# Last head attention: the queries' squares summed by turning them and squaring with ACT's accumulator

## The chip, the cores and the metric

The kernel runs on one core of a Trainium2 chip, in one launch. The metric is the device time of that launch in microseconds (us). The engines are named as in the profile: PE is TensorE (PEld its weight loads), ACT is ScalarE, DVE is VectorE, POOL is GpSimd, SP issues the DMAs.

## The reference, cut to what matters

Four blocks of attention and feed-forward work on `x` of 32 x 64 x 512 and a context of the same size. The change touches the attention of the last block (its names carry the tag 3): 32 heads of 128 columns, 8 pairs of key and value heads, four query heads to each.

```python
def _rmsnorm(x, w):
    xf = x.astype(jnp.float32)
    var = jnp.mean(xf * xf, axis=-1, keepdims=True)
    return (xf * jax.lax.rsqrt(var + EPS)).astype(x.dtype) * w
q = (hidden_states @ Wq.T).reshape(bsz, q_len, H, HD).transpose(0, 2, 1, 3)
k = (cross_attention_states @ Wk.T).reshape(bsz, kv_len, KVH, HD).transpose(0, 2, 1, 3)
q = _rmsnorm(q, q_norm_w)
k = _rmsnorm(k, k_norm_w)
scores = jnp.einsum('bhqd,bhkd->bhqk', q, k) * scale + attention_mask
probs = jax.nn.softmax(scores, axis=-1)
out = jnp.einsum('bhqk,bhkd->bhqd', probs, v)
return out @ Wo.T
```

Each query row needs the sum of the squares of its 128 columns. The kernel folds the two weights of the norms into the keys and multiplies the finished scores of a row by its query's inverse root.

## The kernel before, in words

`phase_heads` runs twice, for the attention of the second block (tag 1, without norm) and for the last one (tag 3, `norm` true). Its outer loop takes four groups of 8 batches. In a group, `heads` goes over 8 key heads, each with four steps t = 0 to 3, so 32 steps n: a pair of query heads takes two steps, one for each half of the 8 batches. The bodies of the first and last key head are written out, those between them are a loop of the hardware. "Third step" below is t = 2, an odd step is t = 1 or 3.

The engines run their own fixed lists and meet by semaphores. PE's list is the one that sets the order. In step n it does, in this order:

- `scores(t)` (L1663), keys times queries for four batches, into bank SBK; two query heads lie in the 128 columns of one piece of `qf`;
- in the third step of all but the last key head `keys(i + 1)`, the next key head's projection (L131 to L133, twelve products);
- `head(n + 2)`, the query projection of a head two steps on, twelve products of 128x512 into bank QB (L131 to L133). ACT then squares QB into `sq` and copies it to `qf` (`head_high`, L1580 and L1581), and `a_q` counts it;
- `turn` (L1679), the previous step's softmax shares turned, which DVE copies to `tf` (L1791);
- `output` of two steps ago, twelve products with the output weights; in the third step it comes before `turn`;
- in odd steps `squares_sum` (L1673): eight products of `sq` with 32 columns of ones, into the free half of bank SBK, one sum of squares for each row of the next pair;
- `values_of` (L1687), the values' products of the previous step into bank AB.

ACT's list in a step: the exponential (L1607), `head_high`, in odd steps the high parts of the next weights (`wqh` L1540, `woh` L1545) and `queries_root` (L118 and L120: logarithm, exponential), then `out_high` (L1585), which takes the values' products. DVE multiplies the scores by the root (L1814), does the softmax (L1816 to L1830) and the low part of the output (`out_low`, L1795). POOL makes the low parts of the weights (L1516, L1520), SP loads them.

The waits around the change are these three, on PE before `scores`, on PE before `squares_sum`, and on DVE before the scaling:

```python
if norm and t % 2 == 0:
    pe.wait_ge(m["a_qrs"], 2 * (i * HP + t // 2) + 1)
pe.wait_ge(m["v_s"], n + 1)
dve.wait_ge(m["a_qrs"], 2 * (i * HP + t // 2) + 2)
```

Of the kernel before, what the change touches and what calls it, by code (L numbers as in the profile page):

```python
# [11 lines left out]
ALU = mybir.AluOpType  # L12
ACT = mybir.ActivationFunctionType
AX_X = mybir.AxisListType.X

P = 128
B, S, D = 32, 64, 512
BG = 8
# [37 lines left out]
def build(nc, a, out):  # L56
    with ExitStack() as top:
# [1344 lines left out]
        def heads(tag, g, NKV, HP, KEYS, norm, wq, wo, wk, vraw, rq, ro, rk, wqh, wql, wkh, wkl, keys_of, queries_of, craw, gate):  # L1402
# [5 lines left out]
            SCALE = float(HD) ** -0.5  # L1408
            names = ("s_q", "a_q", "s_k", "a_ksq", "s_kss", "s_qss", "v_kn", "a_kn", "a_k", "v_in", "s_s",
                     "v_s", "v_m", "a_e", "v_p", "s_t", "v_t", "s_av", "a_o", "v_o", "s_wo", "a_wq", "p_wq",  # L1410
# [3 lines left out]
            PT = 128 * (HB * KEYS // P)  # L1414
            EQ = 32
            with ExitStack() as ph:
                def tb(name, shape, dt=F32):
                    return sb(f"h{tag}_{name}", shape, dt, ctx=ph)
# [9 lines left out]
                if norm:  # L1428
                    sq, ksq, rks, sc = (tb("sq", [P, 2, BG, 2, S]), tb("ksq", [P, TG]), tb("rks", [P, TG]),
                                        tb("sc", [P, HB, KEYS]))  # L1430
                    qrs = tb("qrs", [P, 2, BG])

# [4 lines left out]
                def ring_of(z, n):  # L1437

                    return z[:, n // 2, :, n % 2, :]
# [10 lines left out]
                with nc.Block() as blk:  # L1450
# [80 lines left out]
                    def _(act):  # L1531
# [34 lines left out]

                        def queries_root(k, pair):

                            act.wait_ge(m["s_qss"], k + 1)
                            root(act, qrs[:, pair], ps[:, SBK, HB * KEYS:2 * HB * KEYS].rearrange("p (b e) -> p b e", e=EQ)[:, :, 0],  # L1570
                                 m["a_qrs"], 2 * k, 1.0 / HD, EPS, math.log(SCALE))

# [4 lines left out]
                        def head_high(n, ring):  # L1577
                            act.wait_ge(m["s_q"], n + 1)
                            if norm:
                                nc.scalar.activation(ring_of(sq, ring), by_batch(QB), ACT.Square)  # L1580
                            nc.scalar.copy(ring_of(qf, ring), by_batch(QB)).then_inc(m["a_q"], 1)  # L1581
# [14 lines left out]
                        head_high(1, 1)  # L1596
                        if norm:
                            queries_root(0, 0)

                        def body(i, first, last):  # L1600
                            for t in range(NS):
# [22 lines left out]
                                split_steps(act, i, t, last, kv, q, o)  # L1624
                                if norm and t % 2 and not (last and t == NS - 1):
                                    queries_root(i * HP + (t + 1) // 2, (t + 1) // 2 % 2)
                                if not (first and t == 0):
                                    out_high(n)
                        over_groups(act, body)
                        out_high(NSTEP)  # L1630

                    @blk.tensor
                    def _(pe):
# [33 lines left out]

                        def squares_sum(n, pair):

                            pe.wait_ge(m["a_q"], n + 2)  # L1670
                            for b in range(BG):
                                col = HB * KEYS + EQ * b
                                last = nc.tensor.matmul(ps[:, SBK, col:col + EQ], sq[:, pair, b].rearrange("p h t -> p (h t)"),  # L1673
                                                        ones[:, 0:EQ], start=True, stop=True)
                            last.then_inc(m["s_qss"], 1)

# [31 lines left out]
                        if norm:  # L1708
                            squares_sum(0, 0)

                        def body(i, first, last):
                            for t in range(NS):
# [6 lines left out]
                                if not start:  # L1719
                                    pe.wait_ge(m["v_s" if norm else "a_e"], n)  # L1720
                                if norm and t % 2 == 0:
                                    pe.wait_ge(m["a_qrs"], 2 * (i * HP + t // 2) + 1)
                                scores(t)
# [7 lines left out]
                                if not (last and t >= NS - 2):  # L1731
                                    pe.wait_ge(m["a_q"], n + 2)
                                    if t % 2 == 0:
                                        wait(pe, m["p_wq"], i * HP + t // 2)
                                    head(n + 2, t % 2, (t + 2) % 4, ((t + 2) // 2) % 2)
# [21 lines left out]
                                if not (first and t < 2) and not early:  # L1757
                                    product()
                                if norm and t % 2 and not (last and t == NS - 1):
                                    pe.wait_ge(m["v_s"], n + 1)  # L1760
                                    squares_sum(n + 1, (t + 1) // 2 % 2)
                                if not start:
# [17 lines left out]
                    def _(dve):  # L1780
# [27 lines left out]
                        def largest(i, t, own):  # L1808
                            n = i * NS + t
                            dve.wait_ge(m["s_s"], n + 1)  # L1810
                            if norm:
                                dve.wait_ge(m["a_qrs"], 2 * (i * HP + t // 2) + 2)
                                half = slice(HB * (t % 2), HB * (t % 2) + HB)
                                nc.vector.tensor_tensor(sc[:], kbank(SBK)[:, 0:HB], bc(qrs[:, t // 2 % 2, half]), ALU.mult).then_inc(m["v_s"], 1)  # L1814
                                dve.wait_ge(m["v_s"], n + 1)
# [145 lines left out]
```

## Time and profile before

| | us |
|---|---|
| median of 3 runs | 3870.94 |
| lowest and highest | 3866.55, 3883.64 |
| profiled execution, its own time | 3880.8 |
| its span, first to last instruction | 3879.0 |
| PE busy in the span | 3478.2 |
| ACT busy in the span | 1466.2 |
| mean granted TensorE clock | 0.946 of full |

The profiled execution has a span of 3879.0 us and 1.8 us around it. The last attention occupies the span from about 2409 us to 3797 us: four groups that look alike in the trace, with an entry stage (values of the context, norm of `x`) between them. In the profile a product of fp32 operands shows as two instructions, a turn as one; rows of `h_` names without a tag are of either attention, and the time tells which.

### The profile page before, as it was taken

To read this page: it belongs to the slowest core of one execution; us is meant where nothing else is said; L and a number is where in the kernel's file an instruction comes from. 1 tells how busy PE (TensorE), PEld (TensorE's weight loads), DVE (VectorE), ACT (ScalarE), POOL (GpSimd) and SP (SyncE) were. 2 spreads that over 40 slices of the span, in tenths; PEclk is the share of its full clock that TensorE was granted. 3 is DMA by queue.
4 is the path that set the end of the run, shared out by engine and by line. 5 is a ranking of instruction groups with operands and counts; after the bars stand their busy time and mean duration, and the time that the engine had idled before them with its cause. 6 is when DMAs were issued, how large, how long until landed. Compare 5 with 4: busy or idle time off the path is not lost. (4 is left out here: it accounts for less than half of the span.)

```text
span 3879.0 us, 50267 instructions
## 1 busy us (share of the span) xinstructions
PE 3478.2 (90%) x18456; PEld 2828.8 (73%) x18466; DVE 1768.3 (46%) x3589; ACT 1466.2 (38%) x3218; POOL 937.3 (24%) x515
## 2 busy tenths in 40 slices
PE   6999989799899899979988935999899999989996
PEld 5777775588688778868865723888588778868884
DVE  4677765234333424433443464444344434434444
ACT  3333432344244334434432443343344333433432
POOL 1111102233223223223322312222222222222220
PEclk8899999899999999999998977999999999999998
DMA  2000000221112122112101102210112121111111
GB/s 91 1 1 1 1 1 20 87 71 56 55 62 68 36 71 68 38 66 71 58 22 76 44 3 87 63 60 30 68 60 62 35 73 59 54 54 51 60 40 49
DMA packets 57162, 191.33 MB, mean 49 GB/s; under 512 B 9152, under 2 KB 9920, under 8 KB 53184
## 3 DMA queue, kind: packets, MB, share of 16 engines
q1 hardware_dynamic: 57024, 189.46, 14.5%
q8 instruction: 91, 1.49, 0.2%
q14 instruction: 47, 0.39, 0.0%
HBM read 185.24 MB, written 4.19 MB: 49 GB/s over the span
## 5 line engine op out<-in xcount | busy, mean ns | idle before, releaser
L1795 DVE TENSOR_TENSOR h_ol<-ps,h_oh 128x512 fp32r<-128x512 f32 x256 | 177.1, 692 | 743.2 <-ACT h_oh L1585 743.2
L1516 POOL TENSOR_TENSOR h_wql<-h_rq,h_wqh 128x1024 fp32r<-128x1024 f32 x112 | 276.2, 2466 | 937.7 <-ACT h_wqh L1540 937.7
L131 PE MATMUL ps<-h_woh,h_oh 128*128 128x512 f32 x1024 | 437.0, 427 | 23.5 <-DVE h_ol L1795 23.2
L133 PE MATMUL ps<-h_woh,h_ol 128*128 128x512 f32 x1024 | 405.1, 396 | 0.0
L132 PE MATMUL ps<-h_wol,h_oh 128*128 128x512 f32 x1024 | 403.6, 394 | 0.0
L1520 POOL TENSOR_TENSOR h_wol<-h_ro,h_woh 128x1024 fp32r<-128x1024 f32 x128 | 305.6, 2387 | 187.3 <-ACT h_woh L1545 187.3
L1585 ACT CAST h_oh<-ps 128x512 fp32r<-128x512 f32 x256 | 149.7, 585 | 445.7 <-PE ps L1687 445.7
L1791 DVE COPY h_tf<-ps 128x512 f32<-128x512 f32 (+1 forms) x256 | 142.7, 557 | 347.7 <-PE ps L1679 347.7
L1687 PE MATMUL ps<-h_tf,h_vf 128*128 128x128 f32 x2048 | 279.0, 279 | 17.6 <-DVE h_tf L1791 17.6
L1687 PEld LDWEIGHTS ps<-h_tf,h_vf 128*128 128x128 f32 x2048 | 262.0, 192 | 38.5 <-DVE h_tf L1791 25.2
L1610 ACT ACTIVATE h_ex<-ps,h_mx 128x128 f32<-128x128 f32 x512 | 181.4, 366 | 241.0 <-DVE h_mx L1821 241.0
L1663 PE MATMUL ps<-h_kf,h_qf 128*128 128x128 f32 (+1 forms) x2048 | 267.6, 274 | 4.1 <-ACT h_qf L1581 2.7
L1663 PEld LDWEIGHTS ps<-h_kf,h_qf 128*128 128x128 f32 x2048 | 252.7, 194 | 7.5 <-ACT h_qf L1581 4.4
L131 PEld LDWEIGHTS ps<-h_woh,h_oh 128*128 128x128 f32 x1024 | 192.8, 188 | 71.7 <-DVE h_ol L1795 30.7
L133 PEld LDWEIGHTS ps<-h_woh,h_ol 128*128 128x128 f32 x1024 | 193.2, 189 | 46.6
L132 PEld LDWEIGHTS ps<-h_wol,h_oh 128*128 128x128 f32 x1024 | 193.9, 189 | 42.3 <-issue 6.7
L131 PE MATMUL ps<-h_Hh,h_wqh 128*128 128x512 f32 x512 | 210.6, 411 | 13.9 <-POOL h_wql L1516 11.1
L131 PE MATMUL ps<-h_Xh,h_wqh 128*128 128x512 f32 x512 | 212.0, 414 | 2.5 <-ACT h_qf L1581 2.5
L133 PE MATMUL ps<-h_Xh,h_wql 128*128 128x512 f32 x512 | 204.0, 398 | 0.0
L132 PE MATMUL ps<-h_Xl,h_wqh 128*128 128x512 f32 x512 | 202.9, 396 | 0.0
L133 PE MATMUL ps<-h_Hh,h_wql 128*128 128x512 f32 x512 | 201.4, 393 | 0.0
L132 PE MATMUL ps<-h_Hl,h_wqh 128*128 128x512 f32 x512 | 201.0, 393 | 0.0
(278 smaller groups left out, 6938.3 us busy)
## 6 DMA issues: line engine op xcount, KB each, us to landing
h_rq<-in_L_Wq SPq DMA_DIRECT2D x128, 512.0 KB, 3.6
h_ro<-in_L_Wo SPq DMA_DIRECT2D x128, 512.0 KB, 4.0
h_rk<-in_L_Wk SPq DMA_DIRECT2D x48, 256.0 KB, 2.7
h_craw<-in_ctxT SPq DMA_DIRECT2D x10, 1024.0 KB, 5.5
cnat<-in_ctx SPq DMA_DIRECT2D x4, 1024.0 KB, 11.0
t_craw<-in_ctxT SPq DMA_DIRECT2D x4, 1024.0 KB, 4.9
t_cn<-in_ctx SPq DMA_DIRECT2D x4, 1024.0 KB, 6.1
out_rows<-x SPq DMA_DIRECT2D x16, 256.0 KB, 2.0
```

Source lines behind the costliest of these rows:

```text
L131: nc.tensor.matmul(dst, lh, rh, start=start, stop=False, **kw)
L132: nc.tensor.matmul(dst, lh, rl, start=False, stop=False, **kw)
L133: return nc.tensor.matmul(dst, ll, rh, start=False, stop=stop, **kw)
L1516: nc.gpsimd.tensor_tensor(wql[:, par], rq[:, par], f(wqh[:, par]), ALU.subtract).then_inc(m["p_wq"], 1)
L1520: nc.gpsimd.tensor_tensor(wol[:, par], ro[:, par], f(woh[:, par]), ALU.subtract).then_inc(m["p_wo"], 1)
L1585: nc.scalar.copy(by_head(oh), ps[:, AB, :].rearrange("p (b h t) -> p b h t", h=2, t=S)).then_inc(m["a_o"], 1)
L1610: ins = nc.scalar.activation(ex[:, b], kbank(SBK)[:, b], ACT.Exp, bias=mx[:, 1, b:b + 1], scale=SCALE, accum_out=mx[:, 2, b:b + 1])
L1663: last = nc.tensor.matmul(ps[:, SBK, b4 * KEYS:(b4 + 1) * KEYS], qf[:, pair, b].rearrange("p h t -> p (h t)"), kf[:, b], start=True, stop= ...
L1687: last = nc.tensor.matmul(ps[:, AB, b4 * P:(b4 + 1) * P], vf[:, b], tf[:, c * P:(c + 1) * P], start=True, stop=True)
L1791: nc.vector.tensor_copy(tf[:], ps[:, TBK, 0:PT]).then_inc(m["v_t"], 1)
L1795: nc.vector.tensor_tensor(by_head(ol), ps[:, AB, :].rearrange("p (b h t) -> p b h t", h=2, t=S), f(by_head(oh)), ALU.subtract).then_inc(m[ ...
```

## The change

The sums of squares of the queries are formed in another way, in every step and not in every second one.

- Gone: the Square of 128x512 in `head_high`; `squares_sum` on PE with its two waits; the wait of `scores` for the root.
- New on PE: `turn_queries(t + 1)` in each step between `output` (in the third step: `turn`) and `values_of`. Four transposes put the next step's queries, row by row, into bank QB. Before it PE waits for the copy of `head(n + 2)`.
- New on ACT: `queries_square(n + 1)` at the end of the step, behind `out_high`: four Squares of 128x128 out of QB, each with its sum into one column of `qss`; then `queries_root(n + 1)` on 4 columns.
- New wait on PE: `head(n + 2)` writes QB, so it waits for the four sums of `a_qsq`.
- DVE scales with the root of its own step.

```diff
-                        def queries_root(k, pair):
-
-                            act.wait_ge(m["s_qss"], k + 1)
-                            root(act, qrs[:, pair], ps[:, SBK, HB * KEYS:2 * HB * KEYS].rearrange("p (b e) -> p b e", e=EQ)[:, :, 0],
-                                 m["a_qrs"], 2 * k, 1.0 / HD, EPS, math.log(SCALE))
+                        def queries_square(n, half):
+                            act.wait_ge(m["s_qt"], n + 1)
+                            for b in range(HB):
+                                nc.scalar.activation(sq[:, half, b], ps[:, QB, b * HD:(b + 1) * HD], ACT.Square,
+                                                     accum_out=qss[:, b:b + 1]).then_inc(m["a_qsq"], 1)
+
+                        def queries_root(n, half):
+
+                            act.wait_ge(m["a_qsq"], HB * n + HB)
+                            root(act, qrs[:, half], qss[:], m["a_qrs"], 2 * n, 1.0 / HD, EPS, math.log(SCALE))
...
                         def head_high(n, ring):
                             act.wait_ge(m["s_q"], n + 1)
-                            if norm:
-                                nc.scalar.activation(ring_of(sq, ring), by_batch(QB), ACT.Square)
                             nc.scalar.copy(ring_of(qf, ring), by_batch(QB)).then_inc(m["a_q"], 1)
...
                                 split_steps(act, i, t, last, kv, q, o)
-                                if norm and t % 2 and not (last and t == NS - 1):
-                                    queries_root(i * HP + (t + 1) // 2, (t + 1) // 2 % 2)
                                 if not (first and t == 0):
                                     out_high(n)
+                                if norm and not (last and t == NS - 1):
+                                    queries_square(n + 1, (t + 1) % 2)
+                                    queries_root(n + 1, (t + 1) % 2)
...
-                        def squares_sum(n, pair):
-
-                            pe.wait_ge(m["a_q"], n + 2)
-                            for b in range(BG):
-                                col = HB * KEYS + EQ * b
-                                last = nc.tensor.matmul(ps[:, SBK, col:col + EQ], sq[:, pair, b].rearrange("p h t -> p (h t)"),
-                                                        ones[:, 0:EQ], start=True, stop=True)
-                            last.then_inc(m["s_qss"], 1)
+                        def turn_queries(t):
+
+
+                            for b4 in range(HB):
+                                last = nc.tensor.transpose(ps[:, QB, b4 * P:(b4 + 1) * P],
+                                                           qf[:, t // 2 % 2, HB * (t % 2) + b4].rearrange("p h t -> p (h t)"),
+                                                           ident[:])
+                            last.then_inc(m["s_qt"], 1)
...
-                                if norm and t % 2 == 0:
-                                    pe.wait_ge(m["a_qrs"], 2 * (i * HP + t // 2) + 1)
                                 scores(t)
...
                                     pe.wait_ge(m["a_q"], n + 2)
+                                    if norm:
+                                        pe.wait_ge(m["a_qsq"], HB * n + HB)
...
-                                if norm and t % 2 and not (last and t == NS - 1):
-                                    pe.wait_ge(m["v_s"], n + 1)
-                                    squares_sum(n + 1, (t + 1) // 2 % 2)
+                                if norm and not (last and t == NS - 1):
+                                    if not (last and t == NS - 2):
+                                        pe.wait_ge(m["a_q"], n + 3)
+                                    else:
+                                        pe.wait_ge(m["a_qsq"], HB * n + HB)
+                                    turn_queries(t + 1)
...
-                                dve.wait_ge(m["a_qrs"], 2 * (i * HP + t // 2) + 2)
-                                half = slice(HB * (t % 2), HB * (t % 2) + HB)
-                                nc.vector.tensor_tensor(sc[:], kbank(SBK)[:, 0:HB], bc(qrs[:, t // 2 % 2, half]), ALU.mult).then_inc(m["v_s"], 1)
+                                dve.wait_ge(m["a_qrs"], 2 * n + 2)
+                                nc.vector.tensor_tensor(sc[:], kbank(SBK)[:, 0:HB], bc(qrs[:, t % 2]), ALU.mult).then_inc(m["v_s"], 1)
```

ACT's list in the fourth step of a key head of the loop and the start of the next one, before and with the change (`h_ex` exponential, `h_kf` keys, `h_qf` queries' copy, `h_wqh` and `h_woh` weights, `h_qrs` root, `h_oh` output):

```order
L1607 ACTIVATE h_ex<-h_sc 128x256
L1561 COPY h_kf<-h_kn 128x512
L1578 REGISTER_ALU
L1580 ACTIVATE h_sq<-ps 128x8x64
L1581 COPY h_qf<-ps 128x8x64
L41 ISA
L1540 CAST h_wqh<-h_rq 128x1024
L1545 CAST h_woh<-h_ro 128x1024
L118 ACTIVATE h_qrs<-ps 128x8
L119 REGISTER_ALU
L120 ACTIVATE h_qrs<-h_qrs 128x8
L1585 CAST h_oh<-ps 128x4x2x64
```

```order
L1610 ACTIVATE h_ex<-h_sc 128x256
L1560 COPY h_kf<-h_kn 128x512
L1582 REGISTER_ALU
L1583 COPY h_qf<-ps 128x8x64
L41 ISA
L1539 CAST h_wqh<-h_rq 128x1024
L1544 CAST h_woh<-h_ro 128x1024
L1587 CAST h_oh<-ps 128x4x2x64
L1569 ACTIVATE h_sq,h_qss<-ps 128x128 x4
L1574 ISA
L118 ACTIVATE h_qrs<-h_qss 128x4
L119 ISA
```

The Square in front of the copy of `h_qf` is gone, the root has moved behind `h_oh`, and four Squares with sums stand ahead of it.

PE's list at the same place, from the end of `output` to the first product of the next `head`, before and with the change (here a product counts once; `h_tf` are the turned shares, `h_Xh` the normed rows):

```order
L133 MATMUL ps<-h_woh,h_ol 128x512
L1670 REGISTER_ALU
L1673 MATMUL ps<-ones,h_sq 128x32 x8
L1687 MATMUL ps<-h_tf,h_vf 128x128 x4
L1465 REGISTER_ALU
L1465 COMPARE_AND_BRANCH
L1663 MATMUL ps<-h_kf,h_qf 128x64 x4
L131 MATMUL ps<-h_Xh,h_wqh 128x512
```

```order
L133 MATMUL ps<-h_woh,h_ol 128x512
L1766 REGISTER_ALU
L1676 MATMUL ps<-ident,h_qf 128x128 x4
L1691 MATMUL ps<-h_tf,h_vf 128x128 x4
L1464 REGISTER_ALU
L1464 COMPARE_AND_BRANCH
L1667 MATMUL ps<-h_kf,h_qf 128x64 x4
L131 MATMUL ps<-h_Xh,h_wqh 128x512
```

Four turns stand where the eight narrow products stood; in even steps they are new, with nothing gone. Between the turns and the `head` that overwrites their bank stand the values' products and `scores`.

## Rows read from the trace of the kernel before

**Rows 1.** The page's head and its first part (busy us, share of the span).

```profile
span 3879.0 us, 50267 instructions
...
PE 3478.2 (90%) x18456; PEld 2828.8 (73%) x18466; DVE 1768.3 (46%) x3589; ACT 1466.2 (38%) x3218; POOL 937.3 (24%) x515
```

**Rows 2.** Busy time by stretch: length, PE, PEld, DVE, ACT, POOL, PEclk, DMA share, GB/s.

```profile
2442.00:2700.00 258.00, 254.38 (x1440) 216.38 (x1439) 114.67 (x265) 103.16 (x194) 68.89 (x33) 1.00 0.18 56
...
2420.00:2440.00 20.00, 17.12 (x93) 14.95 (x93) 6.90 (x18) 7.72 (x16) 3.50 (x2) 0.83 0.06 16
```

**Rows 3.** Waits of PE's loads, 2442 to 2700: waiter, releaser, total us, times, longest.

```profile
PEld ps L1687 <- DVE h_tf L1791: 5.3, 7, 0.8
```

**Rows 4.** Timeline of a body step's PE work: start us, us, engine, line, operation.

```profile
2592.63 0.48 PE L131 MATMUL ps<-h_ch,h_wkh 128*128 128x512 f32 x1
...
2595.47 0.39 PE L131 MATMUL ps<-h_Xh,h_wqh 128*128 128x512 f32 x1
...
2603.64 0.97 PEld L1663 LDWEIGHTS ps<-h_kf,h_qf 128*128 128x128 f32 x8
...
2610.20 1.98 PEld L1673 LDWEIGHTS ps<-ones,h_sq 128*128 128x128 f32 x16
...
2612.10 0.97 PEld L1687 LDWEIGHTS ps<-h_tf,h_vf 128*128 128x128 f32 x8
...
2613.00 0.97 PEld L1663 LDWEIGHTS ps<-h_kf,h_qf 128*128 128x128 f32 x8
...
2619.79 1.05 PE L1687 MATMUL ps<-h_tf,h_vf 128*128 128x128 f32 x8
...
2620.57 0.97 PEld L1663 LDWEIGHTS ps<-h_kf,h_qf 128*128 128x128 f32 x8
...
2621.47 0.19 PEld L131 LDWEIGHTS ps<-h_Xh,h_wqh 128*128 128x128 f32 x1
```

**Rows 5.** Timeline of PE's weight loads in the first attention: four turns, next load.

```profile
1306.40 0.58 PEld L1679 LDWEIGHTS ps<-ident,h_pr 128*128 128x128 f32 x4
...
1306.95 0.19 PEld L131 LDWEIGHTS ps<-h_woh,h_oh 128*128 128x128 f32 x1
```

**Rows 6.** ACT: two groups by line (xcount, busy us, mean ns), four timeline rows.

```profile
L118 ACT ACTIVATE h_qrs<-ps 128x8 f32<-128x8 f32 x64 | 11.4, 179 | 43.6 <-PE ps L1673 43.6
...
L1580 ACT ACTIVATE h_sq<-ps 128x512 f32<-128x512 f32 x128 | 75.8, 592 | 76.3 <-PE ps L133 76.0
...
2607.84 0.59 ACT L1580 ACTIVATE h_sq<-ps 128x512 f32<-128x512 f32 x1
...
2608.33 0.57 ACT L1581 COPY h_qf<-ps 128x512 f32<-128x512 f32 x1
...
2610.68 1.04 ACT L1545 CAST h_woh<-h_ro 128x1024 fp32r<-128x1024 f32 x1 [0.84 <-PE ps L133]
...
2620.88 0.59 ACT L1585 CAST h_oh<-ps 128x512 fp32r<-128x512 f32 x1 [2.84 <-PE ps L1687]
```

**Rows 7.** Timeline of ACT in the first attention: exponentials with accumulated sums.

```profile
1305.94 0.37 ACT L1610 ACTIVATE h_ex<-ps,h_mx 128x128 f32<-128x128 f32 x1 [2.05 <-DVE h_mx L1821]
...
1306.29 0.36 ACT L1610 ACTIVATE h_ex<-ps,h_mx 128x128 f32<-128x128 f32 x1
...
1307.23 0.22 ACT L1610 ACTIVATION_READ_ACCUMULATOR h_ex<-ps,h_mx 128x1 f32 x1
```

**Rows 8.** Timeline of PE's weight loads at a group's entry.

```profile
2421.19 1.86 PEld L1673 LDWEIGHTS ps<-ones,h_sq 128*128 128x128 f32 x16 [1.59 <-ACT h_qf L1581]
...
2423.49 1.78 PEld L1663 LDWEIGHTS ps<-h_kf,h_qf 128*128 128x128 f32 x8 [0.44 <-issue]
...
2425.15 0.33 PEld L131 LDWEIGHTS ps<-h_Xh,h_wqh 128*128 128x128 f32 x1
...
2430.06 1.22 PEld L1663 LDWEIGHTS ps<-h_kf,h_qf 128*128 128x128 f32 x8
...
2431.75 0.19 PEld L131 LDWEIGHTS ps<-h_Xh,h_wqh 128*128 128x128 f32 x1 [0.46 <-ACT h_qf L1581]
```

More of the change, by code:

```diff
@@ L1408, in heads @@
             SCALE = float(HD) ** -0.5
-            names = ("s_q", "a_q", "s_k", "a_ksq", "s_kss", "s_qss", "v_kn", "a_kn", "a_k", "v_in", "s_s",
+            names = ("s_q", "a_q", "s_k", "a_ksq", "s_kss", "s_qt", "a_qsq", "v_kn", "a_kn", "a_k", "v_in", "s_s",
                      "v_s", "v_m", "a_e", "v_p", "s_t", "v_t", "s_av", "a_o", "v_o", "s_wo", "a_wq", "p_wq",
@@ L1414, in heads @@
             PT = 128 * (HB * KEYS // P)
-            EQ = 32
             with ExitStack() as ph:
@@ L1428, in heads @@
                 if norm:
-                    sq, ksq, rks, sc = (tb("sq", [P, 2, BG, 2, S]), tb("ksq", [P, TG]), tb("rks", [P, TG]),
+                    sq, ksq, rks, sc = (tb("sq", [P, 2, HB, HD]), tb("ksq", [P, TG]), tb("rks", [P, TG]),
                                         tb("sc", [P, HB, KEYS]))
-                    qrs = tb("qrs", [P, 2, BG])
+                    qss, qrs = tb("qss", [P, HB]), tb("qrs", [P, 2, HB])
                 def values_raw(i, r):
@@ L1597, in _ @@
                         if norm:
+                            queries_square(0, 0)
                             queries_root(0, 0)
@@ L1708, in _ @@
                         if norm:
-                            squares_sum(0, 0)
+                            pe.wait_ge(m["a_q"], 2)
+                            turn_queries(0)
                         def body(i, first, last):
```

## The prediction

> **What bounds the kernel now.** I read four views in this order. The page's first part says that TensorE (PE) is busy 90% of the span [rows 1]. The stretches then say where: inside the last head attention it is busy 254.38 of 258 us at full clock, in one group of batches out of four alike, while ACT is busy only 103 us there [rows 2]. The waits in that stretch leave PE one stall, 5.3 us in 7 times, 0.76 us each, before the values' products in the third step of every head group, until DVE has copied the turned shares [rows 3]. So in this phase the queue of PE is the clock: what PE issues less is gained whole, what ACT does more costs nothing as long as PE doesn't wait for it. The timeline of PE's weight loads gives the pitch. From one `scores` to the next it is 9.36 us in an odd step, which holds `squares_sum`, and 7.57 us in an even one [rows 4].
>
> **What goes away on PE.** A `squares_sum` is 16 instructions (8 products, two passes each). They hold the queue 1.90 us, from 2610.20 to 2612.10. The difference of the two pitches is 9.36 − 7.57 = 1.79 us; I take that, since the values' products behind them start 0.1 us closer [rows 4]. A group of batches has 16 of these: one in the entry, one in step 1, and 14 in steps 3, 5, ... 29. The 14 give back 14 × 1.79 = 25.1 us. In step 1 it stood behind a wait for the copy; without it, and with the copy earlier, I reckon 1.8 us gained there, the new turn included.
>
> **What PE gets.** Each step now turns four 128x128 pieces of the queries. The first attention turns four such pieces in 0.55 us, from 1306.40 to 1306.95 [rows 5]. Behind a large product the next small block starts about 0.1 us closer, as above, so 0.45 us a step. In the seven third steps they fall into the 0.76 us that PE waits anyway [rows 3] and cost nothing; if DVE's copy came sooner they would cost their 0.55. That leaves 22 steps of the body: 22 × 0.45 = 9.9 us.
>
> **What ACT gets, and who waits.** ACT loses one Square of 128x512 per step, 0.59 us [rows 6], and does four Squares of 128x128 with a sum, plus the root in every step and not in every second. ACT has the room. But the order counts: the turned queries lie in the PSUM bank into which the next `head` writes, and PE now waits for all four sums (`a_qsq`) before that `head`. ACT may start the Squares only behind `out_high`, which waits for the values' products. So the chain is: values done, `out_high`, four Squares, `head`; what PE has to do meanwhile is `scores` alone. In numbers, from the row of the values' products: they end at 2619.79 + 1.05 = 2620.84 and the next `head` loads at 2621.47, so PE has 0.63 us of cover behind that end [rows 4]. `out_high` starts 0.04 us after the end [rows 6]. The next ACT operation on its heels starts 0.49 us later, as Square and copy do at 2607.84 and 2608.33 [rows 6].
>
> The four Squares are the unknown. Upper bound: the four exponentials with a sum of the first attention run from 1305.94 to the end of the last accumulator read at 1307.23 + 0.22 = 1307.45, 1.51 us at a pitch of 0.35 [rows 7]. They take their bias from a tensor, the Squares don't. From the rows of ACT's operations out of PSUM without such a bias, 0.179 us for 8 columns and 0.592 for 512 [rows 6], 128 columns lie at 0.179 + 120/504 × 0.413 = 0.28 us. In rows 7 the pitch is about the duration (0.35 against 0.37), so 3 × 0.28 + 0.28 + a last read's end 0.1 later, 1.2 us. That is my value, nearer in kind; lower bound 1.0, if the reads overlap more. The stall is then 0.04 + 0.49 + 1.2 + 0.04 (semaphore to PE) − 0.63 = 1.14, say **1.15 us**; with 1.51 it is 1.45, with 1.0 it is 0.95. The Trainium skill (ScalarE: Activation LUTs, What ACT_TABLE_LOAD costs) says that a bias given as a pointer adds about 93 ns to an ACTIVATE. By that page as an estimate the exponentials' chain less 4 × 0.09 is 1.15 us, and the sum below would come out at about +20 us instead of the +51 us that the exponentials' own row gives.
>
> Which steps pay? A group has 30 `head` calls in its steps. In the seven third steps `keys` stands between `scores` and `head`, 2.84 us of products (2592.63 to 2595.47) [rows 4], more than any bound. Two belong to the entry. 21 pay: 21 × 1.15 = 24.2 us. Other users don't wait longer: the softmax of a step needs the root, about 0.5 us behind the sums, which puts its start 0.5 us behind the start of `head`. Today it starts about 0.7 us behind it, because DVE's `out_low` comes first. The product's split weights have the whole of `head` as cover. In an odd step `woh` starts at 2610.68 and takes 1.04 us [rows 6]; the values' products would end at 2610.20 + 0.55 + 1.2 = 2611.95, so `out_high` is not held, with 0.2 us to spare.
>
> **Entry and end of a group.** At the entry PE waits for the copy of the second head, then sums, and the first `scores` waits for the root. That chain stands at 2421.19, 2423.49 and 2425.15 [rows 8]. Now the copy comes 0.49 earlier, four turns take 0.55, `scores` waits for nothing, and the next `head` waits for the Squares: 2420.70 + 0.55 + 0.2 + 1.2 = 2422.65, 2.5 us sooner. The head after it, 6.6 us behind today (2431.75), gets the whole round trip, copy 0.6, turn 0.55, Squares 1.2 and three handovers, about 1.4 us more. Net −1.1. At the end the last two softmaxes start 1.3 us later, of which the waits for `out_low` that are there today cover all but 0.3.
>
> **Sum.** Per group: −25.1 − 1.8 + 9.9 + 24.2 − 1.1 + 0.3 = +6.4 us; four groups: **+25 us** (25.6). Against the profiled execution's own 3880.8 us that is 3906; the profiled execution is 10 us above the median of the runs, so I put the same difference on the median of 3870.9: **3896 us**, +0.65%. A measurement of this kernel can tell about 0.5%, some 19 us, from no change; the forecast lies just beyond.
>
> **Rivals.**
> *The Squares cost what the exponentials cost* (stall 1.45): 0.3 × 21 × 4 = 25 us more, 3921. For it: the only rows with a sum of this size. Against it: the bias.
> *Not slower: the cover is longer and the entry keeps its clock.* In the entry the clock is granted at half for a while: the stretch from 2420 to 2440 shows 0.83 [rows 2], `scores` takes 1.78 us instead of 0.97, and the twelve products of `head` from 2425.15 to 2430.06 take 4.9 us, where the twelve of `keys` in the body take 2.84 [rows 4, 8]. With turns of 128 columns in place of the 32 column sums, and no wait for the root, PE may stay at 2.4 GHz there. Half clock costs 0.17 × 20 = 3.4 us in that stretch; I count three quarters of it as won back, 2.6 us more per group, an entry of −3.7. With that, the sum is zero at a stall of (25.1 + 1.8 − 9.9 + 3.7 − 0.3)/21 = 0.97, about the lower bound; at 0.95 it is −2 us, 3869. It decides by the Squares' chain: under 1.03 us no loss, over it a loss. For it: the reads may hide; against it: in rows 7 each read holds the next exponential back.
> *The stall is hidden altogether*, if the Squares in fact run beside something PE still has to do: then only the gains are left, 4 × (6.4 − 24.2) = −71, 3800. Against it: the order on both engines.
> *The clock.* Both attentions' bodies are granted the full 2.4 GHz without a break, with 1.8 us of 32 column sums in every second step; with turns and an idle PE instead, it may fall to 1.2 GHz as in the entry, where PE had waited and then run narrow products. One fall costs about 0.17 × 20 = 3.4 us [rows 2]; one per pass over four steps is 28 × 3.4 = 95 us on top of the forecast, 3991. For it: idle time comes to every step. Against it: the first attention turns four pieces a step at full clock, and stalls here are 1.15 us between blocks of wide products. The Trainium skill (TensorE: Matmul & The Clock Gate, Part 4: PE-mode transpose) states that transposes don't count as PE activity the way products do. By that page the turns would be idle time for the clock, next to the stall.
>
> **Numbers.** Chances: forecast 0.50, dear Squares 0.17, not slower 0.20, stall hidden 0.07, clock 0.06. The forecast's own spread (stall 1.0 to 1.3, turns 0.35 to 0.55) is about 13 us each way, so a third of it lies within 0.5%. Slower by over 0.5%: 0.33 + 0.17 + 0.06 = 0.56; within: 0.17 + 0.20 = 0.37; faster: 0.07. The range takes in both bounds of the Squares and leaves out the hidden stall, the clock and some tails: 3870 to 3930.
>
> **What would show it.** In the changed profile: no 128x32 products; 512 more transposes, in blocks of four at about 0.55 us; four Squares of about 0.28 us with reads at a pitch near 0.28; PE waits for them before `head` 21 times in a group for about 1.1 us, and not in the step with `keys`; the even pitch of `scores` near 7.57 + 0.45 + 1.15 = 9.2 us, the odd one the same; granted clock 1.00 in the body. If the waits are under 0.9 us or absent, or if the clock in the body isn't 1.00, the forecast is wrong in that step.

## The result, and the profile after

Over 22 runs of each kernel the medians are 3869.07 us before (3852.31 to 3883.64) and 3885.16 us after (3866.25 to 3896.42). The ratio is 1.0042 with an interval of [1.0028, 1.0055]: 16 us slower. That is less than the 25 us forecast, with its sign and inside its range. One of the five runs of experiment 7 below took 5910 us at a granted clock of 0.55; its cause is open, and the ratio there leaves it out (the median does not).

The two profiled executions can't be subtracted. That of after took 3875.96 us, 4.8 us less than that of before, although the four groups of its last attention are 13.8 us longer together: everything else, which both kernels share, came out 18.6 us shorter. So I compare stretches of the last attention. The page's head and first part, after:

```profile
span 3874.2 us, 50460 instructions
...
PE 3407.7 (88%) x17944; PEld 2744.0 (71%) x17954; DVE 1799.4 (46%) x3589; ACT 1572.2 (41%) x4242; POOL 944.7 (24%) x515
```

PE has 512 matmuls less and is busy 70.5 us less than in [rows 1]. ACT has 1024 instructions more and is busy 106 us more. So PE was given time back, and the kernel is no faster. Groups by line and form say where the time went (count, then busy us, mean ns, then idle time before and what ended it):

```profile
L131 PE MATMUL ps<-h_Xh,h_wqh 128*128 128x512 f32 x512 | 209.9, 410 | 80.3 <-ACT h_sq L1569 76.6 <-issue 3.7
L1569 ACT ACTIVATE h_sq<-ps 128x128 f32<-128x128 f32 x512 | 134.9, 285 | 6.0 <-PE ps L1676 6.0
L1569 ACT ACTIVATION_READ_ACCUMULATOR h_sq<-ps 128x1 f32 x512 | 110.4, 216 | 0.0
```

The product of `head` now stands 76.6 us behind the Squares (L1569), a wait that before did not have. The stretch that answers to [rows 2], and the waits in 2442 to 2700 that answer to [rows 3]:

```profile
2440.00:2700.00 260.00, 241.66 (x1320) 201.45 (x1319) 119.07 (x264) 122.39 (x405) 67.74 (x31) 1.00 0.17 50
```

```profile
PE ps L131 <- ACT h_sq L1569: 16.3, 18, 1.0
...
PEld ps L131 <- ACT h_sq L1569: 12.2, 12, 1.0
PEld ps L131 <- issue: 9.0, 13, 1.1
PEld ps L1691 <- DVE h_tf L1799: 1.9, 6, 0.3
```

PE is busy 93% of this stretch where it was busy 99% of the other [rows 2], at a granted clock of 1.00 in both. Part of the loads' stall is listed as "issue": seven of those 13 times it is the same wait, of 1.0 to 1.1 us ahead of `head`, and the other six are 0.24 us each ahead of `output`, as in before. The old wait for DVE's copy has shrunk from 0.76 us to 0.3 us, since the turns now use up the rest. One step of the body, the `scores` of an odd step (2603.38) with what stands around them, in PE's loads and then in ACT's timeline:

```profile
2601.93 0.59 PEld L1676 LDWEIGHTS ps<-ident,h_qf 128*128 128x128 f32 x4
2602.49 0.97 PEld L1691 LDWEIGHTS ps<-h_tf,h_vf 128*128 128x128 f32 x8
2603.38 0.97 PEld L1667 LDWEIGHTS ps<-h_kf,h_qf 128*128 128x128 f32 x8
2605.37 0.19 PEld L131 LDWEIGHTS ps<-h_Xh,h_wqh 128*128 128x128 f32 x1 [1.01 <-ACT h_sq L1569]
...
2611.02 0.59 PEld L1676 LDWEIGHTS ps<-ident,h_qf 128*128 128x128 f32 x4
```

```profile
2603.69 0.58 ACT L1587 CAST h_oh<-ps 128x512 fp32r<-128x512 f32 x1 [3.77 <-PE ps L1691]
2604.17 0.28 ACT L1569 ACTIVATE h_sq<-ps 128x128 f32<-128x128 f32 x1
2604.34 0.20 ACT L1569 ACTIVATION_READ_ACCUMULATOR h_sq<-ps 128x1 f32 x1
2604.43 0.28 ACT L1569 ACTIVATE h_sq<-ps 128x128 f32<-128x128 f32 x1
...
2605.09 0.23 ACT L1569 ACTIVATION_READ_ACCUMULATOR h_sq<-ps 128x1 f32 x1
```

ACT waits 3.77 us for the values' products, then runs `out_high` first. The four Squares run from 2604.17 to 2605.09 + 0.23 = 2605.32, and 0.05 us later PE loads for `head`. Turned queries had been in the bank since about 2602.5. ACT stood idle while they were ready, because `out_high` comes first in its list.

**Where the 13.8 us are.** From the times at which PE starts `scores`, the stretches of a group of batches (us, mean of the four groups). A group is counted from PE's first products in it (of zeros, L1636 in before) to the end of its last `output`; the values of the context and the norm of `x` between two groups are left out. The first row ends at the `scores` of step 2, each other one at the next `scores`:

| stretch of a group | before | after | after − before |
|---|---|---|---|
| entry, steps 0 and 1 | 28.92 | 23.47 | −5.45 |
| step 2 | 12.44 | 13.23 | +0.8 |
| steps 3 to 29 | 255.81 | 263.22 | +7.4 |
| step 30 | 5.36 | 5.81 | +0.45 |
| from there to the end of the group | 15.62 | 15.86 | +0.24 |
| group | 318.14 | 321.59 | +3.4 |

The four groups of after agree within 0.1 us (321.55 to 321.61). Those of before don't: 318.14, 316.51, 316.57 and 321.35. They differ by the clock. In 18 us at the entry it was 0.81, 0.91, 0.91 and 0.81, and in the fourth group it fell once more in steps 1 and 2:

```profile
3500.00:3518.00 18.00, 16.92 (x74) 14.35 (x75) 5.19 (x13) 6.99 (x14) 5.89 (x3) 0.81 0.23 73
```

There step 2 takes 13.91 us, in the other three groups 11.95. Against those three the change costs 1.3 us in step 2, and the +0.8 is a mean with a group in which the clock of before had fallen. The kernel of experiment 4, whose PE list is that of before, lacks this second fall in its profile; its groups are 0.85 us shorter in the mean. From them the change costs 4.3 us a group, 17 us in all. So the 13.8 us are known to about 3 us.

In the body the pitches of `scores` are 9.10 in odd steps (9.37 before), 9.18 in even ones (7.57) and 11.93 in the third (11.94).

Two stretches differ from the forecast: the entry gained more, and step 2 lost something. At the entry, after:

```profile
2402.05 0.42 PEld L1676 LDWEIGHTS ps<-ident,h_qf 128*128 128x128 f32 x4 [1.10 <-ACT h_qf L1583]
2402.44 0.97 PEld L1667 LDWEIGHTS ps<-h_kf,h_qf 128*128 128x128 f32 x8
2404.00 0.19 PEld L131 LDWEIGHTS ps<-h_Xh,h_wqh 128*128 128x128 f32 x1 [0.59 <-issue]
...
2407.71 0.42 PEld L1676 LDWEIGHTS ps<-ident,h_qf 128*128 128x128 f32 x4 [1.10 <-ACT h_qf L1583]
```

`scores` takes 0.97 us, not 1.78, and the twelve products of `head` end within 2.7 us, not 4.9 [rows 8]. The stretches of 18 us around the first group's entry give the clock as 0.81 in before and 1.00 in after:

```profile
2418.00:2436.00 18.00, 15.16 (x67) 12.33 (x65) 6.84 (x17) 5.26 (x13) 0.00 (x0) 0.81 0.09 38
```

```profile
2400.00:2418.00 18.00, 15.23 (x88) 12.34 (x87) 9.11 (x20) 10.66 (x40) 4.09 (x3) 1.00 0.14 50
```

In step 2, after (POOL, DVE, ACT and PE in the order of their starts):

```profile
2417.69 2.39 POOL L1519 TENSOR_TENSOR h_wol<-h_ro,h_woh 128x1024 fp32r<-128x1024 f32 x1
...
2418.29 2.07 DVE L1823 TENSOR_TENSOR h_sc<-h_sc,mask 128x256 f32<-128x256 f32 x1
...
2421.31 0.42 ACT L1610 ACTIVATE h_ex<-h_sc 128x256 f32<-128x256 f32 x1 [3.58 <-DVE h_sc L1825]
...
2422.32 0.30 PEld L1655 LDWEIGHTS ps<-h_ksq,ones 128*128 128x128 f32 x2 [1.45 <-issue]
```

The mask addition takes 2.07 us where its neighbours of the same size take 0.42. It ends 0.28 us behind the end of POOL's instruction (2420.36 and 2420.08). Behind it the exponential is late, behind that ACT's work on the keys (L1579), and PE waits 1.45 us. Before had the same hold in its first three groups, earlier against PE's work (the addition ends 4.05 us behind the start of the step's `scores`, after 5.72), and no wait of PE behind it. Its first group:

```profile
2440.05 2.40 POOL L1520 TENSOR_TENSOR h_wol<-h_ro,h_woh 128x1024 fp32r<-128x1024 f32 x1
...
2440.68 2.06 DVE L1816 TENSOR_TENSOR h_sc<-h_sc,mask 128x256 f32<-128x256 f32 x1
```

### The profile page after: what moved, and what is told of

It reads as the page before. It is cut to its first block and busy times, and to the rows that moved or that the text cites. A ratio compares the mean times of both kernels' runs of the same rounds, so it can differ in the third digit from the quotient of the medians.

```text
span 3874.2 us, 50460 instructions
## 1 busy us (share of the span) xinstructions
PE 3407.7 (88%) x17944; PEld 2744.0 (71%) x17954; DVE 1799.4 (46%) x3589; ACT 1572.2 (41%) x4242; POOL 944.7 (24%) x515
## 5 line engine op out<-in xcount | busy, mean ns | idle before, releaser
L1515 POOL TENSOR_TENSOR h_wql<-h_rq,h_wqh 128x1024 fp32r<-128x1024 f32 x112 | 282.5, 2522 | 932.9 <-ACT h_wqh L1539 932.9
L131 PE MATMUL ps<-h_Xh,h_wqh 128*128 128x512 f32 x512 | 209.9, 410 | 80.3 <-ACT h_sq L1569 76.6
L131 PE MATMUL ps<-h_Hh,h_wqh 128*128 128x512 f32 x512 | 210.8, 412 | 13.8 <-POOL h_wql L1515 11.1
L1544 ACT CAST h_woh<-h_ro 128x1024 fp32r<-128x1024 f32 x128 | 133.9, 1046 | 179.0 <-PE ps L133 162.2
```

The lines of the kernel that those rows point to most:

```text
L131: nc.tensor.matmul(dst, lh, rh, start=start, stop=False, **kw)
L1515: nc.gpsimd.tensor_tensor(wql[:, par], rq[:, par], f(wqh[:, par]), ALU.subtract).then_inc(m["p_wq"], 1)
L1544: nc.scalar.copy(woh[:, par], ro[:, par]).then_inc(m["a_wo"], 1)
```

## The experiments

Theory: the body's loss is one wait per step, for a chain that begins with `out_high`, and the gain lies at the entry, where the clock stays up. Rivals: ACT's added work or the turns cost by themselves; the bank is what costs, in whatever order ACT works; the entry gained only because a wait is gone.

**1. The Squares ahead of `out_high`.**

```diff
+    queries_square(n + 1, (t + 1) % 2)
     out_high(n)
-    queries_square(n + 1, (t + 1) % 2)
     queries_root(n + 1, (t + 1) % 2)
```

> The changed kernel with one move: ACT does the four Squares ahead of out_high and the root behind it. Theory A (the loss is the round trip: out_high, Squares, then head, with only scores as cover; 1.1 us in each of 21 steps of a group): the Squares now run beside the values' products, the wait of PE before head goes in even steps and falls to about 0.3 us behind an odd step, where the cast of woh comes first; 4 x 21 x 1.1 = 92 less about 17 left over, so 75 us less than the changed kernel's 3885, about 3810, ratio to before 0.985. Pitch of scores 8.0 us where the step before was even, 8.3 where it was odd. Theory B (the loss is the extra work itself, turns on PE and ACT's load): no move, ratio stays at 1.004.

Measured: 3807.91 us (5 runs), 0.9833 [0.9812, 0.9855] of the 3873.85 of before. Odd pitch 8.02, even 8.35, third unchanged at 11.93, a group 301.2 us. PE's loads in an even step and at the start of the next, then ACT's timeline:

```profile
2623.60 0.97 PEld L1668 LDWEIGHTS ps<-h_kf,h_qf 128*128 128x128 f32 x8
2624.85 0.19 PEld L131 LDWEIGHTS ps<-h_Xh,h_wqh 128*128 128x128 f32 x1 [0.28 <-issue]
...
2631.97 0.97 PEld L1668 LDWEIGHTS ps<-h_kf,h_qf 128*128 128x128 f32 x8
2632.86 0.19 PEld L131 LDWEIGHTS ps<-h_Xh,h_wqh 128*128 128x128 f32 x1
```

```profile
2631.38 0.28 ACT L1569 ACTIVATE h_sq<-ps 128x128 f32<-128x128 f32 x1 [2.82 <-PE ps L1677]
...
2632.30 0.22 ACT L1569 ACTIVATION_READ_ACCUMULATOR h_sq<-ps 128x1 f32 x1
2632.40 0.60 ACT L1587 CAST h_oh<-ps 128x512 fp32r<-128x512 f32 x1
```

The Squares now run beside the values' products and `scores`, and in the odd step `head` starts 0.89 us after `scores`, with no wait. The move of two lines takes 77 us off the change by the medians, 81 us by the two ratios and by the traces (4 × 20.4). Of the 23.1 us that a group had lost in its 21 steps (1.10 us each, worked out below), 21.0 came back; what is left is the 0.28 us in even steps, where the cast of `woh` stands ahead of the Squares. Step 30 is 0.7 us longer than in after (6.51 against 5.81). So nearly the whole loss in the body was the order on ACT, not the amount of its work. A second measurement on another chip gave the same:

> sq_first again beside pool_pieces on one chip, to tell their 5 us apart: theory (step 2 is 1.27 us shorter in pool_pieces, nothing else differs) gives pool_pieces a ratio lower by 0.0013; the rival gives none.

Measured: 3809.33 us (6 runs), 0.983 [0.9792, 0.9868].

**2. Every Square twice.**

```diff
+    for b in range(HB):
+        nc.scalar.activation(sq[:, 1 - half, b], ps[:, QB, b * HD:(b + 1) * HD], ACT.Square,
+                             accum_out=spare[:, b:b + 1])
     for b in range(HB):
         nc.scalar.activation(sq[:, half, b], ...
```

> The changed kernel with each set of four Squares done twice on ACT (the first set into a spare sum). Theory A (ACT's chain between out_high and head is exposed in full in 21 steps of a group): 4 more at 0.25 us are 1.0 us a step, 84 us in all, ratio to before about 1.026; the third step, where keys covers, stays at 11.93 us. Theory B (the waits are a handover of fixed length and ACT has room): under 10 us.

Measured: 4049.65 us (4 runs), 1.0445 [1.0424, 1.0465], more than expected. The size per Square was as expected: a paying step grows by 1.04 us (9.18 to 10.2 at t = 0, 9.10 to 10.17 at t = 1), and the third step stays at 11.93. That is about 22 us of the 41 that a group grew by. Most of the rest goes with the clock. A stretch of the body, and one step's load with its wait:

```profile
2780.00:3080.00 300.00, 259.61 (x1269) 204.91 (x1268) 108.38 (x238) 149.05 (x581) 72.71 (x35) 0.95 0.18 55
```

```profile
2860.18 0.19 PEld L131 LDWEIGHTS ps<-h_Xh,h_wqh 128*128 128x128 f32 x1 [2.13 <-issue]
```

At 2.1 us of idle time in three of four steps the granted clock in the body is 0.95, no longer 1.00, and in most passes over the four steps the pitch at t = 3 becomes 11.7, now and then the one at t = 0 too, where 10.2 shows without a fall: 1.5 us. The entries fell too, to 0.91, 0.75, 0.74 and 0.91 over 18 us. So the mechanism of the prediction's clock rival exists, and the change's own body, with 1.1 us of idle time in three of four steps, doesn't meet it.

**3. Every turn twice.**

```diff
-    for b4 in range(HB):
+    for b4 in 2 * list(range(HB)):
         last = nc.tensor.transpose(ps[:, QB, ...
```

> The changed kernel with the four turns of the queries done twice in each step. Theory A (PE's queue is full, a turn costs its load's pitch of 0.14 us): 0.56 us in 22 steps, 0.25 us in the seven third steps where 0.32 us of idle time is left, and the entry twice 0.56: 15 us a group, 60 us in all, ratio to before about 1.020. Theory B (turns fall into the time that PE waits for ACT anyway): near 0, ratio 1.004.

Measured: 3940.12 us (4 runs), 1.0151 [1.0123, 1.0178]. In the trace the four groups are 45 us longer than in after, where 60 was expected: four more turns cost 0.43 us in a step that pays (9.10 to 9.53), not 0.56, and 0.11 in the third, not 0.25. In the block of eight:

```profile
2605.31 1.03 PEld L1676 LDWEIGHTS ps<-ident,h_qf 128*128 128x128 f32 x8
2606.30 0.97 PEld L1691 LDWEIGHTS ps<-h_tf,h_vf 128*128 128x128 f32 x8
```

A block of four holds the queue 0.56 us, one of eight 0.99, so a further turn costs 0.11 us. The turns are a real cost with the size that the prediction gave them, and no second stall hangs on them.

**4. ACT's work alone, in the kernel before.** Four Squares with sums of `ident` behind `out_high`, and the root in every second step more; nobody waits for them.

```diff
     out_high(n)
+    for b in range(HB):
+        nc.scalar.activation(spsq[:, t % 2, b], ident[:], ACT.Square,
+                             accum_out=spare[:, t % 2, b:b + 1]).then_inc(m["a_x"], 1)
+    act.wait_ge(m["a_x"], HB * n + HB)
+    if t % 2 == 0:
+        root(act, spq[:, t // 2], spare[:, 0], m["a_y"], ...)
```

> The kernel before with ACT's new work alone: behind out_high of each step four Squares of 128x128 with sums, of the identity and into spare tiles, and a root in even steps too; nobody waits for them. Theory A (ACT's added load costs nothing, only who waits for it does): ratio 1.000, pitches of scores 7.57, 9.37 and 11.94 us as before. Theory B (ACT's load holds its other operations back): 0.3 us or more a step, 30 us or more.

Measured: 3872.56 us (10 runs) beside 3873.85, 0.9999 [0.9976, 1.0023]; the pitches are those of before to 0.01 us (7.57, 9.37, 11.94). ACT is busy 1638.0 us in this profile, 172 us more than in before and 66 more than in after, and that is free as long as nobody waits for it. With experiment 1 this excludes the first rival.

**5. The turned queries in another bank.** ACT's list is the change's own; the turns go to bank TBK, and PE waits for the Squares before `keys` and before `turn` instead of before `head`. Before `turn_queries` it waits for DVE's copy of TBK.

```diff
-    ps[:, QB, b4 * P:(b4 + 1) * P]
+    ps[:, TBK, b4 * P:(b4 + 1) * P]
```

> The changed kernel with the turned queries in the bank of the turned shares instead of the bank of head; head no longer waits for the Squares, but keys (third step), the next turn of shares and, for DVE's copy, the turn of the queries do. ACT's order stays (out_high first). Theory A (what costs is that the next head overwrites the bank): pitches of scores 8.02 us in three of four steps instead of 9.1; the third step now pays the 1.1 us before keys and about 0.5 us behind DVE's copy, 13.5 instead of 11.93. 37.6 instead of 39.3 us for four steps, 12 us a group, about 48 us less than the changed kernel's 3885, ratio to before 0.992. Theory B (ACT's order alone costs, whoever overwrites what): ratio stays at 1.004.

Measured: 3834.27 us (6 runs), 0.9916 [0.9891, 0.9941] of the 3871.18 of before. Pitches 8.01 and 8.26, the third 13.49. Two waits of a third step, in PE's loads:

```profile
2610.78 0.19 PEld L131 LDWEIGHTS ps<-h_ch,h_wkh 128*128 128x128 f32 x1 [1.02 <-ACT h_sq L1569]
...
2621.00 0.42 PEld L1676 LDWEIGHTS ps<-ident,h_qf 128*128 128x128 f32 x4 [0.82 <-issue]
```

In odd and even steps `head` now covers the Squares and the stall is gone. The 0.24 us that an even step still takes over an odd one are another wait, for POOL's low part of the query weights (L1515), which `head` reads. It ends 0.06 us before `head` loads:

```profile
2628.99 2.36 POOL L1515 TENSOR_TENSOR h_wql<-h_rq,h_wqh 128x1024 fp32r<-128x1024 f32 x1 [16.48 <-ACT h_wqh L1539]
```

```profile
2630.29 0.97 PEld L1667 LDWEIGHTS ps<-h_kf,h_qf 128*128 128x128 f32 x8
2631.41 0.19 PEld L131 LDWEIGHTS ps<-h_Xh,h_wqh 128*128 128x128 f32 x1
```

In the third step it stands before `keys`, which uses the same bank, and a second one comes with DVE's copy. So it is a matter of how much work PE has between the turns and the next writer of their bank. Either more of it or an earlier Square cures it; the earlier Square of experiment 1 costs 0.7 us a group in step 30 and nothing in the third step.

**6. The entry, in three kernels.** The narrow products put back, with nobody waiting for them:

```diff
     pe.wait_ge(m["a_q"], 2)
+    for b in range(BG):
+        col = HB * KEYS + 32 * b
+        nc.tensor.matmul(ps[:, SBK, col:col + 32], ...qf[:, 0, b]..., ones[:, 0:32], start=True, stop=True)
     turn_queries(0)
```

> The changed kernel with eight 128x32 products of the queries with ones (results unused) ahead of the first turn at each group's entry, as squares_sum stood there. Theory A (the entry kept its full clock because these narrow products and the wait for the root are gone): the clock at the entry falls to half again, the first step's pitch goes from 5.65 to 6 us or more and the stretch shows PEclk under 1; the group grows by more than the products' 1.9 us. Theory B (the clock there is chance or hangs on what came before): only 1.9 us a group, PEclk 1.00.

The wait of the first `scores` for the root put back:

```diff
+    if norm and start:
+        pe.wait_ge(m["a_qrs"], 2)
     scores(t)
```

> The changed kernel with the old wait alone: the first scores of a group wait for the root of the first queries. Theory A (idle time at the entry lets the clock fall): first pitch over 6 us and half clock in at least some groups, plus about 2 us of waiting a group. Theory B (the narrow products alone do it): 2 us a group of waiting, clock 1.00.

And both:

> The changed kernel with both, the eight narrow products and the wait for the root at a group's entry. If they act together, as in the kernel before, half clock shows at all four entries; if only chance decides, at some.

Measured, one execution each: 3890.32, 3891.40 and 3901.88 us. A single total can't tell these apart, but a group's time in the trace can (us; the body's steps 3 to 29 are 263.2 to 263.7 in the first four kernels of the table, 255.8 in before):

| kernel | the four groups | granted clock in 18 us at the entry |
|---|---|---|
| after | 321.6 in each | 1.00 in each |
| products back | 324.9, 325.4, 323.8, 323.8 | 0.91 in the first two, 1.00 in the last two |
| wait back | 324.5 in each | 0.91 in each |
| both back | 327.2 in each | 0.81 in each |
| before | 318.1, 316.5, 316.6, 321.4 | 0.81, 0.91, 0.91, 0.81 |

The windows' lines behind it, of the kernel with the products (first and third group), with the wait, and with both:

```profile
2400.00:2418.00 18.00, 15.57 (x89) 12.85 (x88) 7.86 (x18) 8.22 (x29) 1.30 (x2) 0.91 0.07 29
3129.00:3147.00 18.00, 15.22 (x95) 12.71 (x94) 8.23 (x19) 9.30 (x32) 2.38 (x2) 1.00 0.07 27
```

```profile
2403.00:2421.00 18.00, 13.92 (x75) 11.22 (x73) 7.69 (x18) 8.58 (x29) 1.67 (x2) 0.91 0.05 19
```

```profile
2406.00:2424.00 18.00, 14.32 (x70) 11.48 (x68) 5.18 (x14) 5.96 (x26) 0.00 (x0) 0.81 0.06 23
```

Either of the two alone lowers the clock at least in some groups, both together bring it down to 0.81 in all four, which before shows in two. In the profiles of after and of experiments 1, 3, 5 and 7, which have neither, all entries kept 1.00. So PE stays at 2.4 GHz here because both are gone, the wait and the narrow products; in the kernels of this experiment that rests on four entries in one execution of each. Putting them back costs a group 2.2 to 5.6 us, their own time included. What the clock alone costs can be read in the kernel with the products, whose groups differ by it: step 0 takes 6.81 and 7.24 us where the clock fell to 0.91, and 5.64 where it stayed, 1.2 to 1.6 us.

**7. POOL's instruction in pieces.** Experiment 1 with the weights' low part of step 1 in four pieces of 256 columns:

```diff
+    if norm and type(n) is int and n == 1:
+        for h in range(2):
+            for c in range(2):
+                k = slice(256 * c, 256 * c + 256)
+                ins = nc.gpsimd.tensor_tensor(wol[:, par, h, k], ro[:, par, h, k], f(woh[:, par, h, k]), ALU.subtract)
```

> The kernel sq_first with POOL's subtraction of the second product weights in the first key head cut into four pieces of 256 columns. Theory A (in step 2 DVE's mask addition, 2.07 us instead of 0.43, is held until POOL's 2.39 us instruction ends, and PE waits for what follows): the addition takes 1 us or less and the pitch of step 2 falls from 13.2 to about 12 us, 5 us in all, ratio to before 0.982. Theory B (DVE's operation is slow there for another reason): 2 us again, pitch 13.2.

Measured: step 2 falls from 13.22 to 11.96 us, a group from 301.2 to 299.95. POOL's and DVE's timelines:

```profile
2410.52 3.27 POOL L1523 TENSOR_TENSOR h_wol<-h_ro,h_woh 128x256 fp32r<-128x256 f32 x4
...
2411.17 0.42 DVE L1831 TENSOR_TENSOR h_sc<-h_sc,mask 128x256 f32<-128x256 f32 x1
```

The mask addition runs 0.42 us beside POOL's 3.27 us, and PE's wait is gone. That is worth 5 us over the four groups in the trace, although the four pieces take POOL longer than the one instruction did, and it is below what the totals can tell: 3802.77 us (5 runs), 0.9837 [0.9794, 0.9881]. A second measurement, beside experiment 1:

> pool_pieces again beside sq_first_b: ratio to before 0.982, 5 us less than sq_first_b, if the four shorter steps reach the end; the same time if they don't.

Measured: 3793.81 us (6 runs), 0.9801 [0.9763, 0.9839], beside 0.983 [0.9792, 0.9868] for experiment 1 on the same chip. The intervals overlap; that the pieces gain in the total is not shown, that they remove the hold in step 2 is. With either version the kernel beats both before and the change: 1.7 to 2% under before and 2 to 2.4% under the change.

## Why the prediction was right, and where it missed

- **What bounds the kernel.** Right. PE's queue is the clock: 172 us more of ACT are free where nobody waits for them (experiment 4), and turns that hold the queue 0.43 us longer make the pitch 0.43 us longer (experiment 3).
- **The products that go, 14 × 1.79.** Right. With the turns at 0.45 and without a stall the odd pitch is 9.37 − 1.79 + 0.45 = 8.03; experiment 1 shows 8.02.
- **The turns, 0.45 in the step.** Right, by the same pitch. In even steps 7.57 + 0.45 = 8.02 stands against 8.26 in experiment 5 and 8.35 in experiment 1, with a wait ahead of `head` in both: for POOL's part of the weights in experiment 5, for the Squares behind the cast of `woh` in experiment 1.
- **The stall, 21 × 1.15.** Right in place and size. It is 9.10 − 8.03 = 1.07 in odd steps and 9.18 − 8.02 = 1.16 in even ones, mean 1.10. The Squares' chain is 2605.32 − 2604.17 = 1.15 us, not 1.2, since their pitch is 0.25 and not 0.28. The third step doesn't pay, as forecast. Steps 3 to 29 came to +7.4 per group; the terms give 21 × (0.45 + 1.15) − 25.1 = +8.5.
- **Entry and step 1: the term that was mis-sized.** The prediction put −1.1 and −1.8, together −2.9. The traces show −5.45, so 2.5 us per group or 10 us in all were missed. I took the instructions one by one at the speed at which before ran them, and left the granted clock to a rival. Step 1 was right: 8.5 us before, at full clock in the second and third group, and 6.55 after. The −1.1 of the entry was right too but for the clock: in these two groups the stretch up to the `scores` of step 1 is 2.4 us shorter, and of that their fall to 0.91 is worth 1.2 to 1.6 us, an estimate from experiment 6. The rival's entry with step 1, −3.7 − 1.8 = −5.5, is the measured mean, in part by luck: it took the first group's lower clock for all four, where the groups gained 5.9, 4.3, 4.3 and 7.2 us, the fourth with its second fall. The rival's other half, a stall of 0.95, is not what was measured.
- **Step 2: a term that was missing, +0.8 in the mean, +1.3 where before ran it at full clock.** The softmax of step 1 is late now and falls under POOL's instruction in a place where PE waits for what follows. The hold is in the trace of before too, with nobody waiting behind it; I costed the later softmax only at a group's end.
- **The ends.** Step 30 +0.45 as forecast, the tail +0.24 against 0.3.

With the measured values the sum is 7.4 − 5.45 + 0.8 + 0.45 + 0.24 = +3.4 per group and +13.8 for the four, and 16 us in the totals, interval 11 to 21. The forecast of 25 had the stall right, and was too high by the entry. It came within 9 us of the totals partly by luck: the two terms that it missed, the clock at the entry and the hold in step 2, have opposite signs. At 16 us, under the 19 that bound "within 0.5%", it was that case that held, to which I gave 0.37 against 0.56 for slower by more.

Of the other rivals: dear Squares fell at 1.15 against 1.51 us. A hidden stall fell, and experiment 1 shows what it would have been worth: the prediction's 3800 us for that case against a measured 3808. The clock falling in the body didn't occur at 1.1 us of idle time in three of four steps, and did at 2.1. The Trainium skill (TensorE: Matmul & The Clock Gate, Part 4: PE-mode transpose) states that transposes don't count as activity of PE the way products do; in the body here that made no difference, as 1.00 was granted with four turns in each step and a stall in three of four.

## What to carry to other kernels

When an engine hands a shared bank back to the engine that sets the pace, what counts is the chain from the last work it waits for to the release, and not how busy it is. List what stands between in its in-order queue: here one 0.48 us copy ahead of the release, a copy that itself waits for products which end later than the turns that were ready, turned a gain of some 65 us into a loss of 16. And cost a stretch that runs at the lower clock at both clocks: taking a wait out of it can give back more than the wait.

## What the runs showed of the hardware

- **A VectorE addition is held by a GpSimd instruction until that one ends.** With both inputs in SBUF, 128x256 takes 2.07 us beside a GpSimd subtraction of 2.39 us, which it outlasts by 0.28 us, and 0.42 us without, or when the latter is cut in four. The Trainium skill (SBUF — State Buffer, Who interferes with whom) states that a DVE instruction with two SBUF inputs contends with a GpSimd instruction that reads SBUF; this trace agrees, and the pieces (3.27 us in all, the addition 0.42) show that the length of the single GpSimd instruction is what counts.
- **TensorE's granted clock at an entry depends on small things.** With the wait for the root or with eight narrow products it fell to 0.91 over 18 us, with both to 0.81; with neither it stayed at 1.00, except where the Squares were done twice and PE waited longer there (0.74 to 0.91). With the products alone it differed between groups of the same program.
- **Idle time in a steady loop.** 1.1 us in three of four steps, of 9 us each, left the clock at 1.00; 2.1 us in three of four, of 10 us each, brought it to 0.95.
- **Squares with a sum.** Four of 128x128 out of PSUM run at a pitch of 0.25 us, below the 0.285 us of one, and take 1.15 us with the last read; exponentials with a bias from a tensor run at 0.35 [rows 7].
